# Head attention head by head over all tokens, with the real turn between depths as diagonal products on TensorE

## The reference, cut to what matters

```
qkv = query @ W_qkv.T + b_qkv ;  q, k, v as (B, S, 8 heads, 64)
qq, kq, vq = each head's vector / its length * exp(1j * phase)
def _entangle(state, gates):                      # state: 8 heads; for q and for k
    for depth in range(3):
        theta, phi = gates[depth, :7] ; s1 = state[:, :, :-1] ; s2 = state[:, :, 1:]
        ctrl = |s1|**2
        rot = cos(theta/2) * s2 + sin(theta/2) * exp(1j*phi) * conj(s2)
        new = ctrl * rot + (1 - ctrl) * s2
        state = concatenate([new, state[:, :, -1:]], axis=2)
for c in range(4):                                # circuits
    pattern = einsum('bsid,bsjd->bsij', conj(q_ent), k_ent) * constants of c
    probs = softmax(|pattern|**2 * 64**-0.5) ; amps = sqrt(probs + 1e-12)
    weighted = einsum('bsij,bsjd->bsid', amps, vq) ; clip its size, take its sign, add up over c
return real(sum).reshape(B, S, E) @ W_out.T + b_out
```

## Time and profile before

| | us |
|---|---|
| median of 3 runs | 3117.55 (3110.91 to 3119.19) |
| the profiled execution | 3107.78 |
| its span | 3105.7 |
| the head attention in it | 2637 to 2926 |

### The profile page before, as it was taken

How to read it: one execution, slowest core, us unless ns; L and a number is a source line. 1 busy time by engine, 2 the same in 40 slices (tenths; PEclk the granted TensorE clock), 3 DMA queues, 4 the chain that set the end, 5 groups by cost and what they waited for, 6 DMA issues and landing times. The chain is left out here.

```text
span 3105.7 us, 42385 instructions
## 1 busy us (share of the span) xinstructions
PE 2831.7 (91%) x17657; PEld 1527.4 (49%) x17657; DVE 1631.0 (53%) x1937; ACT 1062.4 (34%) x1643; POOL 243.9 (8%) x325
## 2 busy tenths in 40 slices
PE   6999999998989999989999999999999995827899
PEld 3334444443434444456665666666666662515453
DVE  5358999994655666633434343434343333376310
ACT  3254343432424343332323233333232320483210
POOL 1000000000000655400000000000000000000000
PEclk9999999999999999999999999999999997858899
DMA  5033343234424444355655555556565442120203
GB/s 201 28 124 94 90 134 111 86 97 151 132 82 151 131 126 140 98 139 114 148 115 148 115 148 114 148 115 148 115 148 118 111 98 60 51 61 7 109 14 135
DMA packets 487334, 345.85 MB, mean 111 GB/s; under 512 B 246788, under 2 KB 451909, under 8 KB 482536
## 3 DMA queue, kind: packets, MB, share of 16 engines
q1 hardware_dynamic: 487144, 343.15, 40.7%
HBM read 230.79 MB, written 54.62 MB: 92 GB/s over the span
## 5 line engine op out<-in xcount | busy, mean ns | idle before, releaser
L1841 PE MATMUL ca_p_s<-early_halves,ca_qw 128*128 128x448 f16 (+2 forms) x1408 | 467.4, 332 | 1.4 <-DVE ca_qw L1964 1.4
L1842 PE MATMUL ca_p_s<-early_halves,ca_qw 128*128 128x448 f16 (+2 forms) x1408 | 467.5, 332 | 0.0
L1843 PE MATMUL ca_p_s<-early_halves,ca_qw 128*128 128x448 f16 (+2 forms) x1408 | 467.4, 332 | 0.0
L1964 DVE TENSOR_TENSOR ca_qw<-ca_p_w,ca_qw 128x512 f16<-128x512 f32 x128 | 88.4, 690 | 508.4 <-ACT ca_qw L1911 508.4
L394 PE MATMUL vw_pv<-vw_wv,vw_ctx 128*128 128x512 f16 (+1 forms) x688 | 263.8, 383 | 37.2 <-PEq L74 15.1
L395 PE MATMUL vw_pv<-vw_wv,vw_ctx 128*128 128x512 f16 (+1 forms) x688 | 263.3, 383 | 0.0
L396 PE MATMUL vw_pv<-vw_wv,vw_ctx 128*128 128x512 f16 (+1 forms) x688 | 263.0, 382 | 0.0
L1911 ACT ACTIVATE ca_qw<-ca_p_w 128x512 f16<-128x512 f32 x128 | 76.4, 597 | 506.3 <-PE ca_p_w L1822 506.3
L1842 PE MATMUL ca_p_s<-ca_ctx,ca_qw 128*128 128x448 f16 (+2 forms) x640 | 216.2, 338 | 0.0
L1841 PE MATMUL ca_p_s<-ca_ctx,ca_qw 128*128 128x448 f16 (+2 forms) x640 | 216.1, 338 | 0.0
L1843 PE MATMUL ca_p_s<-ca_ctx,ca_qw 128*128 128x448 f16 (+2 forms) x640 | 216.1, 338 | 0.0
(11 more groups left out here) (552 smaller groups left out, 5385.3 us busy)
## 6 DMA issues: line engine op xcount, KB each, us to landing
ca_stage<-in_ctx_t SPq DMA_DIRECT2D x97, 512.0 KB, 3.5
vd<-vw_vst SPq DMA_DIRECT2D x192, 256.0 KB, 2.3
ca_vals<-vd SPq DMA_DIRECT2D x64, 768.0 KB
vw_ring<-in_ctx_t SPq DMA_DIRECT2D x89, 512.0 KB, 3.9
ex_w_d<-in_w_d SPq DMA_DIRECT2D x8, 2048.0 KB, 7.4
vw_ring<-in_w_kv SPq DMA_DIRECT2D x16, 512.0 KB, 4.5
early_r<-state_rows SPq DMA_DIRECT2D x8, 1024.0 KB, 7.8
early_r<-in_w SPq DMA_DIRECT2D x2, 4096.0 KB, 12.6
```

The lines of the kernel that those rows point to most:

```text
L1841: nc.tensor.matmul(o, a[:, 0, c, :], x[:, 0, c, lo:hi], start=(c == 0), stop=False)
L1842: nc.tensor.matmul(o, a[:, 0, c, :], x[:, 1, c, lo:hi], start=False, stop=False)
L1843: last = nc.tensor.matmul(o, a[:, 1, c, :], x[:, 0, c, lo:hi], start=False, stop=(c == CC - 1))
L1964: nc.vector.tensor_tensor(qw[f % 2][:, 1, c, :], p_w[:, :].rearrange("p (c n) -> p c n", n=P), qw[f % 2][:, 0, c, :], ALU.subtract).then_i ...
```

## The change

Partitions now hold (tile parity, feature): partitions 0 to 63 the 64 features for tokens of tiles 0 and 2, partitions 64 to 127 for tiles 1 and 3. q and k lie side by side along the free axis: group indices 0 to 15 are q, 16 to 31 are k. So one instruction on one head covers all tokens of q and k, 512 elements, and q and k are already on the same partitions.

- **Inputs.** The bias comes in four DMAs in place of one; `ld_s` is waited for at 96 in place of 48, six DMAs. All 16 transposes come first, into four banks; DVE and ACT copy two banks each (ACT behind its `Exp` for `sup`).
- **Projections.** `project(i)` does 16 matmuls of 128 x 64 weights on 256 tokens, with the two partition halves of the output in turn. `norm(i)`, `spread_norm(i)`, `length` and `inverse` run once over 512 columns. `leave(i)` has four passes of 256.
- **Recurrence.** Everything is head by head, 512 elements in one instruction. ACT runs `squares` two items ahead of `factors` (`LEAD`). DVE does `product(m)`, then for the next item `turned` (imaginary part alone) and `summed_squares`. The real part is made by TensorE: `turn_state` multiplies `s_im` with a diagonal of tangents and adds `s_re` by the identity, into one of three banks, which `product` reads. POOL makes the 12 diagonals. POOL's four copies for the last head go.
- **Scores.** No DMAs and no copies; ACT writes a negated real part of k (`negative`, 256 elements for each head). `score(h, v)` does 16 matmuls of K = 64 on 128 columns, partition halves in turn, into two banks. `score(1, 0)` is queued ahead of `peaks(0)`.

```diff
-            sp.dma_start(b_qk[:, :], io.b_qk).then_inc(ld_s, 16)
+            for s in range(2):
+                for a in range(2):
+                    sp.dma_start(b_qk[a * DH:(a + 1) * DH, s, :], io.b_qk[s * DH:(s + 1) * DH, :]).then_inc(ld_s, 16)
...
-                for c in range(DC):
-                    last = nc.tensor.matmul(raw_bank(u), w_qk[:, c, i, :],
-                                            xt[:, c, a * HN:(a + 1) * HN], start=(c == 0), stop=(c == DC - 1))
+                for s in range(2):
+                    for c in range(DC):
+                        for a in range(2):
+                            last = nc.tensor.matmul(raw_bank(i)[a * DH:(a + 1) * DH, s * HN:(s + 1) * HN],
+                                                    w_qk[:, c, i, s * DH:(s + 1) * DH],
+                                                    xt[:, c, :].rearrange("p (k a n) -> p a k n", a=2, n=P)[:, a, :, :],
+                                                    start=(c == 0), stop=(c == DC - 1))
...
+            def turn_state(g, i):
+                m = rot(g, i)
+                if m >= len(TURN_BANKS):
+                    b_g, b_i = divmod(m - len(TURN_BANKS), NU - 1)
+                    pe.wait_ge(s_done, 2 * gate(b_g + 1, b_i) + 1)
+                pe.wait_ge(s_done, 2 * (gate(g - 1, i + 1) + 1))
+                o = bank(TURN_BANKS[m % len(TURN_BANKS)])
+                nc.tensor.matmul(o, turns_d[:, m, :], s_im[:, :, i + 1, :], start=True, stop=False)
+                nc.tensor.matmul(o, k.ident[:, :], s_re[:, :, i + 1, :], start=False, stop=True).then_inc(re_turned, 1)
...
+                    for i, (left, right) in enumerate(kinds):
+                        for a in range(2):
+                            rows_a = slice(a * DH, (a + 1) * DH)
+                            last = nc.tensor.matmul(bank(score_bank(m, a))[:, g * P:(g + 1) * P],
+                                                    left[rows_a, HG + at, :, :].rearrange("p h t -> p (h t)"),
+                                                    right[rows_a, at, :, :].rearrange("p h t -> p (h t)"), start=(i == 0),
+                                                    stop=(i == 1))
...
-            for u in range(8):
-                score(0, u)
+            for v in range(4):
+                score(0, v)
+            score(1, 0)
             peaks(0)
...
+            for m in range(len(items) + LEAD):
+                if m < len(items):
+                    squares(*items[m])
+                if m >= LEAD:
+                    factors(*items[m - LEAD])
+                if m == NU + 1:
+                    last_state()
+                    value_squares(0)
+                    value_squares(1)
+                if m == NU + 3:
+                    value_squares(2)
+                    value_squares(3)
+                if m == NU + 5:
+                    value_length()
...
+            for m, (g, i) in enumerate(items):
+                if g == 0 and i + 4 < NH:
+                    normed(i + 4)
+                product(g, i)
+                if m + 1 < len(items) and items[m + 1][0]:
+                    turned(*items[m + 1])
+                    summed_squares(*items[m + 1])
+                if m == NU + 1:
+                    value_sum(0)
+                    value_sum(1)
+                if m == NU + 3:
+                    value_sum(2)
+                    value_sum(3)
+                if m == NU + 6:
+                    value_norm(0)
+                if m == 2 * NU + 1:
+                    value_norm(1)
...
-            copies(0)
-            copies(1)
...
...
             store(0)
             turn(0)
-            move(0)
             store(1)
-            move(1)
             turn(1)
```

More of the change, by code:

```diff
@@ L2283, in _, with turn_x @@
         def _(pe):
[L2284 to L2288, removed]
+            def turn_x():
+                for t in range(NT):
+                    pe.wait_ge(xn_ready, t + 1)
                     for c in range(DC):
[L2290 to L2291 removed]
+                        last = nc.tensor.transpose(bank(XT_BANKS[c])[:, t * P:(t + 1) * P], xn[:, t, c * P:(c + 1) * P],
+                                                   k.ident[:, :])
@@ L2482, in length, with leave @@
-            def length(a):
-                act.wait_ge(n_ready, NH * (a + 1))
-                nc.scalar.activation(root[:, a * HN:(a + 1) * HN], norm_bank(a),
-                                     ACT.Sqrt).then_inc(root_done, 1)
-            def squares(a, g):
+            def leave(i):
+                act.wait_ge(p_ready, 4 * (i + 1))
+                for s in range(2):
+                    v = raw_bank(i)[:, s * HN:(s + 1) * HN]
+                    nc.scalar.activation(n[:, s * HG:(s + 1) * HG, i, :], by_group(v), ACT.Identity,
+                                         bias=b_qk[:, s, i:i + 1]).then_inc(raw_done, 1)
+                    if i >= 2:
+                        act.wait_ge(n_ready, i - 1)
+                    nc.scalar.activation(sqn[i % 2][:, s * HN:(s + 1) * HN], v, ACT.Square,
+                                         bias=b_qk[:, s, i:i + 1]).then_inc(sq_done, 1)
@@ L2554, in _ @@
-            length(0)
-            leave(1, NH // 2)
-            for i in range(NH // 2 + 1, NH):
-                leave(1, i)
-            length(1)
-            squares(0, 0)
-            factors(0, 0)
-            last_state(0)
-            value_squares(0)
-            value_squares(1)
-            squares(1, 0)
-            factors(1, 0)
-            last_state(1)
-            act.wait_ge(sup_ready, 1)
-            for i in range(2):
-                for c in range(CIRC):
-                    nc.scalar.activation(sup_d[:, i, c, :], k.ident[:, :], ACT.Copy,
-                                         scale=sup[:, 2 + i, c:c + 1]).then_inc(diag_done, 1)
@@ L2572, in _ @@
-            for g in range(1, DEPTH):
-                squares(0, g)
-                squares(1, g)
-                if g == DEPTH - 1:
-                    value_length()
-                factors(0, g)
-                factors(1, g)
-                if g == 1:
+            for i in range(1, NH):
+                leave(i)
+            length()
+            LEAD = 2
+            items = [(g, i) for g in range(DEPTH) for i in range(NU)]
+            for m in range(len(items) + LEAD):
[8 more added lines that the diff above has]
+                if m == NU + 3:
@@ L2584, in _ @@
+                if m >= 2 * NU + LEAD + 3:
+                    negative(m - 2 * NU - LEAD - 3)
+            negative(NU)
+            for i in range(len(items) + LEAD - 2 * NU - LEAD - 3, NU):
+                negative(i)
             act.wait_ge(vt_ready, NT)
+            act.wait_ge(s_done, 2 * NU * DEPTH)
             nc.scalar.activation(vsign, bank(6), ACT.Sign).then_inc(vsign_done, 1)
```

355 lines of the change are left out of this document (154 added, 201 removed).

## The result

Before and after were run 19 times each: 3110.84 us median before, 3100.35 after. The ratio is 0.9968, with a 95% interval of 0.9958 to 0.9979: a gain of 10 us, 7 to 13. A second measurement of the same changed kernel gave 0.9974 (0.9963 to 0.9986), 8 us. The forecast was 3112 us, range 3104 to 3148.

A forecast was written before the change was run, and what follows sets the result against it. PE bounds the projections, ACT the first depth, then DVE and ACT take turns. First score +1.9 and scores -7.0 make -5.1: 3102.7 against the profiled 3107.8, plus the median's 9.8 gives 3112 us, range 3104 to 3148.

The forecast's parts named there:

- the anchor: Whole kernel: the shown median lies 9.8 us above the profiled execution's 3107.8, and this was added to the sum.
- `turn_state` is hidden: Depths two and three: its two matmuls, 3.4 us at the low clock, may start three items, 12.7 us, ahead.
- Start: +2.0: Before the first projection: later bias loads 1.5 us and a second bank copy on DVE 0.6; bounds 0 and 3.
- Projections: a head every 5.0: Projections: overlapping half-width matmuls 3.84 us, norm 0.97, width changes 0.2 for each head; 40.1 for eight.
- First depth: 23.3: First depth of the recurrence: ACT is the bound at 23.3 us, its pass of 512 elements taking 0.81.
- The rival with 0.63: ACT's wide pass costs 0.63 us, 21 pairs save 0.34 each, 7.1: 3105; chance 0.10.
- The relay: 4.22 an item: Depths two and three: DVE's 2.54 and ACT's 1.65 us alternate with 0.03 to hand over; 66.8 in all.
- Scores: -7.0: Scores: DVE-bound steps with row halves overlapping, +1.5 in the first part and -8.5 in the rest.
- that rival: Scores: row halves do not overlap, a PE step takes 3.7 us, -0.5 in place of -7.0: 3119; chance 0.15.
- Mixing unchanged: Mixing behind the scores: the change leaves it as it was.
- the first rival: Projections: half-width f32 products do not overlap, +30.7 us; 3143, or 3150 if the scores don't either; chance 0.30.

The follow-up runs named there:

- run 19: Not a label of a run: part of "run 19 times each", the kernels before and after the change, medians 3110.84 and 3100.35 us.
- blocks of eight: Changed kernel with a head's eight projection products of one column half, then eight of the other: 1.0041 of before; a separate kernel, row halves likewise in `score`: 1.0042.
- blocks of four: Changed kernel with a head's projection products ordered four of one column half, then four of the other, in place of in turn: 1.0001 of before.

## Why the prediction was wrong, by its own steps

Two steps failed: the anchor, which put the result outside the range, and the claim that `turn_state` is hidden, the one error of mechanism. The price of the projections was too high by a miscounted term, and hid the second error in the sum.

- **The anchor.** "The median shown is 9.8 us above that, and I add the difference to it." With 19 runs the median is 3.1 above the profiled execution, so 6.7 of the 11.6 us by which 3112 was too high are this step; without them the range would have begun at 3097.3 and held 3100.35. The profile's own sum, 3102.7, was nearer. Of the other 4.9, 2.1 are the stage (7.2 against 5.1), and 2.8 are not located. Three runs that spread over 8 us don't fix a median to a few us.
- **Start: +2.0.** It was -0.5. The last small load was issued 2.2 us later (forecast 1.5), but it landed 3.9 us behind its issue where it had taken 7.1 before, so DVE's wait ended no later. In the other profiles of this layout that time is 3.9 to 6.2, and the first projection comes at 8.1 to 10.3 of the common point; the old layout has 7.1 and 6.7. So the later issue is partly made up in the landing, and what makes the landing quicker is open; the real change lies between -0.5 and +1.8, and the low bound of 0 was about right.
- **Projections: a head every 5.0.** The overlap that was read off f16 rows holds in f32 (4.57; blocks of eight show what it hides). What was too high is the 3.84: it is eight times 0.48, from 1.92 us for four products, and of those 1.92 the records' own pitch explains 8 x 0.216 = 1.73; the other 0.19 belongs to the change of width to the norm and back. So the changes were counted in the products' price, in the norm's 0.54, and once more as 0.2. That 0.2 was itself near: 0.25 is lost (above), which agrees with the rule of the Trainium skill that was weighed here (TensorEngine Tiling (Array Packing), Tiling Modes, Key Properties: a change of the tiling mode drains TensorE). Eight heads at 4.57 in place of 5.0 give 3.4. With the rest of the tail, start of projections to inverse is 43.6 against 48.3.
- **First depth: 23.3.** 23.7, with the wide pass at the 0.81 that was taken. The rival with 0.63 is out. That the sum fits is in part luck: up to the first pair it took 5.4 us in place of 4.0, since `spread_norm` ran at the low clock, and from there 18.2 in place of 19.3.
- **"`turn_state` is hidden".** This is the step that failed in the mechanism: 4.9 us bare, once. The argument compared its length with the lead that its inputs give, and left out what stands ahead of it on its own queue: eight `spread_norm`, 12.5 us, which at the granted clock of 0.50 take 1.71 each, and then three `values`, 15.6 us, the first of them in part at that clock too. The prediction had named this wait as what would break the step. With it depths two and three are 71.6 against 66.8.
- **The relay: 4.22 an item.** 4.27 to 4.28. Reading it off the two queues was right: with the order turned round the items went by at 2.6 and the first score came 15 to 17 us sooner. That the relay is all there is to these depths but for the wait is borne out: 71.6 less 4.9 is 66.7.
- **Scores: -7.0.** -8.1 and -7.9, 31.8 and 32.0 us against 39.8. Row halves overlap; DVE's idle time behind `pattern(0)` is 1.6 in the first profile (under 3 forecast) and 2.1 in the second. The order of the queue is 3 of the 8. The page of the Trainium skill that was named beside that rival (TensorE: Matmul & The Clock Gate, LDWEIGHTS (loading the stationary operand)) would have a step near 3.5 by its rule alone; a warm step took 1.8, and the loads of the two row halves start within 0.01 us of each other and last 0.19 each, so they go beside each other. That a load goes by its columns and not by its rows is not contradicted.
- **Mixing unchanged.** 101.2 against 100.2. The second profile of the changed kernel has 101.2 too, and the old layout with the two scores first 100.1, so this 1 us is probably real; its cause was not looked for.

Together: -2.5 (start), -4.7 (projections), +0.4, +4.8 (the wait), -1.0 (scores), +1.0 (mixing) against the forecast's -5.1 is -7.1, the stage's -7.2. That the forecast of the stage was within 2 us is luck: the projections' error and the wait's cancelled. The chances gave too much to the first rival, for which no row spoke.

## What to carry to other kernels

When an engine works "two items ahead" of another, look at what its input is queued behind: here one sum behind one product made two engines take turns, and moving two calls up brought the first score 15 to 17 us forward, where the rewrite as it stood had gained 5 to 7 us in the stage. The kernel before had no such relay (both engines were busy for some 50 of 56 us); the rewrite made it. For a product said to be hidden, add up everything ahead of it on its own queue at the clock that holds there, not only its own length. And tie a forecast to a ratio or to many runs, since three runs can put the median off by more than the change that is forecast (6.7 us against 5.1 here).

## What the runs showed of the hardware that was not expected

- An f32 product on half the columns (64 of 128, 256 tokens) costs about 0.44 us in line, as long as one on all 128, and at a border between the two column halves 0.80 us is hidden, nearly two products. Products of the other half then start before earlier ones of the same queue; between row halves the names show it (blocks of eight: `ha_s_re,ha_s_im` of the next step at 2797.69, the last of the step before at 2798.33). Sixteen products on the two column halves take 3.60 alternating, 4.63 in blocks of four, 6.24 in blocks of eight.
- A change of width between f32 products can be seen: the norm starts 0.31 us behind the last record of a projection, where records start every 0.216, and a head loses 0.25 us at its two changes.
- PE busy for 99% of 28 us with row halves in line, and the granted clock at 0.50 all along; with the halves in turn it rose about 6 us behind the first score. It was 0.50 as well for 13.7 us from the products with 16 rows (`spread_norm`) on, though PE was busy throughout.
- POOL took 0.58 us (twelve in a row) and 0.74 us (eight in a row) for a 128 x 128 diagonal, and for a pass of 256 once 0.85 and three times 1.89 us, where ACT took 0.30 and 0.40. Spans on POOL are rough.
